# A graph layer's edge stage on blocks of 128 nodes instead of 64, one block per turn

## The chip, the core and the metric

The kernel runs on one core of a Trainium2 chip. A core has five engines that run side by side, each with its own queue of instructions: TensorE (PE, matmuls; PEld is its weight load), VectorE (DVE), ScalarE (ACT), GpSimd (POOL) and SyncE (SP), which here only issues DMAs. They wait for each other on semaphores. SBUF is the memory that the engines work from, PSUM holds what TensorE makes, HBM is the large memory outside. The metric is the device time of the whole program in microseconds (us).

## What is computed

A graph has 6250 nodes of 256 values, and 206250 edges sorted by their target `dst`. The layer is, cut to what matters here:

```python
h = (xn @ W.T).reshape(n, 8, 32)                       # xn: layernorm of x
alpha = sum(h[src] * a_src) + sum(h[dst] * a_dst)      # per edge and head
enc = relu(edge_attr @ edge_W.T + edge_b)
alpha = leaky(alpha + sum(enc * h[dst]))
ex = exp(alpha - segment_max(alpha, dst)[dst])
gnn = segment_sum(h[src] * ex / segment_sum(ex, dst)[dst], dst) + bias
x = x + gnn + mix(xn)                                  # mix: a linear attention over all nodes
out = x + experts(layernorm(x))                        # 8 experts of three layers, a softmax gate
```

## The kernel before

The program is unrolled and runs in stages, with all engines meeting between them.

**start** (`stage_start`): layernorm, h, and the plan of the edges. Per tile of 128 nodes SyncE stores the rows of h with their source scores to HBM (`src_rows`, L351) and two halves of `parts` (`dst_parts`, L358), in which h is split into three bf16 parts, so that bf16 matmuls give it back exactly. The plan cuts the sorted edges into groups of 256 (GE) and the nodes into blocks; a step is one group against one block, and where a group runs over a block's end the step is repeated for the next block.

**kv and mix**: the linear attention. In between GpSimd gathers some of the edges' rows ahead of time.

**edges** (`stage_edges`): 452 turns (D) of 512 edges. A turn d belongs to window d // 8. In turn tau the engines do, each in the order written here:

- TensorE: `spread_out(tau)`, h[dst] for 512 edges into `ps_d`, from the block's `table` and the one-hot matrix `hot` (L1652: the third bf16 part, 64 rows; L1656: the first two parts, 128 rows); `encode(tau+1)`, the edge features (L1641); `aggregate(tau-12)`; `reduce(tau)`, the sum over a head's 32 values (L1669).
- VectorE: `multiply(tau)` (L1837, two halves), the next `hot` (L1826), `weigh(tau-11)` (L1920, the rows by their exponentials), and `add(tau-12)` (L1913, into `sums`). In the first four turns of a window also the softmax work of the window before: scores, two scans, the chain of running maxima, the shift, the rescaling.
- ScalarE: `rectify(tau+1)` (L1734), `put_back(tau-12)` (L1787), the source scores (L1745), the exponentials into the rows (L1771), and the one-hot matrices `hot_e` of 128 edges by 64 nodes for the aggregation (L1779, L1781).
- GpSimd gathers the rows of the sources (L1629), SyncE loads tables, relative indices and features.

A block has 64 nodes (WN), so `sums` has 98 blocks, and each is two partial sums, one on the lower 64 partitions and one on the upper. A turn may meet two blocks, one for each of its two steps (`sub`). So a turn loads two tables, and its aggregation is in two parts. For step 0, unless the turn opens a window, TensorE first copies the block's sums into PSUM with an identity matmul (L1688), accumulates on them, and ScalarE copies the result back (L1787). For step 1 VectorE adds (L1913). The matmuls of a step write partitions 0 to 63 and 64 to 127 (L1692). The order is kept by one counter, `added`: the aggregation of a turn waits for both sums of the turn before, and the add of step 1 for the copy back of step 0.

**combine** (`stage_combine`, the head of the last part): per tile TensorE adds the partial sums (`band_sum`, L2223) of two blocks into one tile of 128 nodes. VectorE divides by the denominators (L2063, L2068, L2073), adds the rest (L2082) and takes the statistics (L2086); ScalarE normalises; TensorE turns the tile (L2207) and makes the router's logits (L2213), 21 tiles later. The experts' weights are loaded into the place of `sums` once it is read.

**experts** (`stage_experts`): dense matmuls.

## Time and profile before

| | us |
|---|---|
| median of 3 runs | 4003.45 (4001.85 to 4003.85) |
| the profiled execution, first to last instruction | 4846.5 |
| of it: start (0 to 190) | 190 |
| kv and mix (190 to 1038) | 848 |
| edges (1038 to 3704) | 2666 |
| combine (3704 to 3827) | 123 |
| experts (3827 to 4847) | 1020 |

### The profile page before, as it was taken

The numbers are of one execution on the slowest core, as the hardware profiler recorded it, in microseconds if no ns is written. First come the engines' busy times: TensorE is split into PE (matmuls) and PEld (weight loads), VectorE is DVE, ScalarE is ACT, GpSimd is POOL, SyncE is SP. The second block draws the span as 40 slices with busy tenths as digits, with TensorE's granted clock in tenths as the row PEclk, the third lists the DMA queues.
The fourth block names the chain that finished last, engine by engine and source line by source line (L and its number), as shares of the span: only waits on it lengthen the run. The fifth ranks groups of instructions, "written<-read, shape, count | busy, mean of one in ns | idle before, by whom it ended". The sixth has DMA issues, their size and how long they took to land. (4 is left out here: it accounts for less than half of the span.)

```text
span 4846.5 us, 80424 instructions
## 1 busy us (share of the span) xinstructions
PE 4087.7 (84%) x22764; PEld 1897.1 (39%) x22765; DVE 2700.2 (56%) x5470; ACT 2291.3 (47%) x6074; POOL 1780.1 (37%) x1859
## 2 busy tenths in 40 slices
PE   5699988957888887788887878878887999999999
PEld 3333322312333333333333333333333666666666
DVE  7566723336666666676666666667666333333333
ACT  4444445524555555555555555555554433333332
POOL 3255555644454445444444444445440000000000
PEclk8799989976888888888888887888887799999999
DMA  7555556655555555555555555555552100000000
GB/s 216 160 165 162 164 177 201 210 156 154 161 168 165 158 165 164 162 168 168 159 162 152 163 157 161 162 159 168 164 162 67 61 8 1 8 8 8 8 8 8
DMA packets 378173, 629.74 MB, mean 130 GB/s; under 512 B 83912, under 2 KB 245063, under 8 KB 377536
## 3 DMA queue, kind: packets, MB, share of 16 engines
q1 hardware_dynamic: 277266, 356.80, 23.4%
q0 software_dynamic: 93408, 257.23, 19.5%
q10 hardware_dynamic: 7104, 11.01, 0.7%
q8 instruction: 179, 2.93, 0.2%
q14 instruction: 216, 1.77, 0.1%
HBM read 520.59 MB, written 104.12 MB: 129 GB/s over the span
## 5 line engine op out<-in xcount | busy, mean ns | idle before, releaser
L1629 POOL DMA_INDIRECT s_rows<-scratch_src_rows,s_idx_w x1312 | 1257.6, 959 | 1367.6 <-PE s_ps_a L1692 563.3
L1837 DVE SCALAR_TENSOR_TENSOR s_enc<-s_enc,s_a_dst,s_ps_d 128x512 f32<-128x512 f32 x904 | 634.9, 741 | 313.3 <-DMA p_feats<-in_edge_f,p_tcol_i 160.8
L1734 ACT ACTIVATE s_enc<-s_ps_f 128x1024 f32<-128x1024 f32 x452 | 459.5, 1017 | 516.6 <-remote 265.5
L1692 PE MATMUL s_ps_a<-s_rows,s_hot_e 128*64 128x264 f32 x3616 | 647.1, 490 | 44.9 <-DVE s_rows L1920 32.4
L2285 DVE SCALAR_TENSOR_TENSOR kx_y_all<-e_ps_o,kx_gate,kx_y_all 128x256 f32 (+1 forms) x392 | 173.5, 480 | 684.2 <-PE e_ps_o L2340 684.2
L1920 DVE TENSOR_TENSOR s_rows<-s_rows,s_ps_x 128x1024 f32<-128x1024 f32 x452 | 545.7, 1207 | 13.6 <-ACT s_a_w L1765 8.7
L1688 PE MATMUL s_ps_a<-ke_sums,k_ident 128*128 x790 | 341.0, 520 | 217.1 <-DVE ke_sums L1913 123.6
L1913 DVE TENSOR_TENSOR ke_sums<-s_ps_a,ke_sums 128x264 f32 x509 | 218.3, 429 | 505.3 <-remote 263.9
L1669 PE MATMUL s_ps_s<-s_enc,s_head_sum 128*32 128x256 f32 x3616 | 353.7, 469 | 152.9 <-DVE s_enc L1837 121.2
L1779 ACT ACTIVATE s_hot_e<-k_iota_row,s_rel_w 128x64 f32<-128x64 f32 x1808 | 480.5, 339 | 0.0
L1787 ACT COPY ke_sums<-s_ps_a 128x264 f32 x395 | 148.6, 376 | 552.5 <-remote 337.8
L2299 ACT ACTIVATE ke_sums<-e_ps,kx_b,kx_g 128x448 f32<-128x448 f32 x224 | 162.1, 724 | 512.9 <-PE e_ps L2319 512.9
L1692 PEld LDWEIGHTS s_ps_a<-s_rows,s_hot_e 128*64 128x64 f32 x3616 | 263.0, 163 | 360.2 <-issue 264.5
L2319 PE MATMUL e_ps<-kx_xT,ke_sums 128*128 (+1 forms) x896 | 347.9, 542 | 6.2 <-PEq L180 6.2
L2340 PE MATMUL e_ps_o<-ke_sums 128*128 128x256 f32 x1568 | 347.6, 379 | 0.0
L2329 PE MATMUL e_ps<-ke_sums 128*128 128x448 f32 x896 | 345.9, 539 | 0.0
L1641 PE MATMUL s_ps_f<-s_feat,k_w_rows 30*128 30x512 bf16 x904 | 304.0, 419 | 27.7 <-DMA s_feat<-scratch_step_parts 14.6
L1656 PE MATMUL s_ps_d<-s_hot,s_table 128*128 128x256 bf16 x1808 | 321.7, 308 | 0.0
L2340 PEld LDWEIGHTS e_ps_o<-ke_sums 128*128 128x128 f32 x1568 | 297.7, 190 | 58.6 <-issue 20.9
L1091 POOL DMA_INDIRECT n_rows<-scratch_src_rows,n_idx x248 | 235.0, 947 | 207.0 <-PE n_ps_g L948 107.5
L1195 POOL DMA_INDIRECT m_rows<-scratch_src_rows,m_idx x248 | 235.7, 951 | 174.7 <-issue 64.6
L1688 PEld LDWEIGHTS s_ps_a<-ke_sums,k_ident 128*128 128x128 f32 x790 | 139.0, 220 | 373.5 <-issue 370.6
(280 smaller groups left out, 5259.0 us busy)
## 6 DMA issues: line engine op xcount, KB each, us to landing
s_table<-scratch_dst_parts SPq DMA_DIRECT2D x904, 96.0 KB
s_rows<-scratch_pre_rows SPq DMA_DIRECT2D x124, 528.0 KB
s_relb<-scratch_rel_rows SPq DMA_DIRECT2D x226, 256.0 KB
scratch_pre_rows<-n_rows SPq DMA_DIRECT2D x62, 528.0 KB
scratch_pre_rows<-m_rows SPq DMA_DIRECT2D x62, 528.0 KB
s_rows<-scratch_src_rows,s_idx_w POOLq DMA_INDIRECT x1312
s_feat<-scratch_step_parts SPq DMA_DIRECT2D x226, 54.0 KB
s_pen_w<-scratch_pen_rows SPq DMA_DIRECT2D x228, 48.1 KB
```

The source lines that it names most:

```text
L1629: pool.indirect_dma_start(out=rows[:, d % R, m, :], out_offset=None, in_=scr["src_table"], in_offset=bass.IndirectOffsetOnAxis(ap=idx_w[:, ...
L1656: last = PE.matmul(ps_d[:, c, sub * GE:(sub + 1) * GE], table[:, u, sub, c * P:(c + 1) * P], hot[:, v, sub * GE:(sub + 1) * GE], start=Fal ...
L1669: last = PE.matmul(ps_s[32 * b:32 * (b + 1), :], head_sum[:, 28 - 4 * k:60 - 4 * k], enc[:, d % 2, c, sub * GE:(sub + 1) * GE], start=(k = ...
L1688: PE.matmul(ps_a[:, 0, 0:SRC_W], keep["ident"][:], sums[:, bass.ds(j, 1), :].rearrange("p o w -> p (o w)"), start=True, stop=False, skip_g ...
L1692: last = PE.matmul(ps_a[t * WN:(t + 1) * WN, sub, 0:SRC_W], hot_e[:, d % 3, 2 * sub + t, :], rows[:, d % R, 2 * sub + t, :], start=(sub == ...
L1734: A.activation(enc[:, d % 2], ps_f[:], ACT.Relu).then_inc(enc_made, 1)
L1779: A.activation(hot_e[:, d % 3, m, :], keep["iota_row"][:, 0:WN], ACT.Abs, bias=rel_w[:, w % 3, k * TD + m:k * TD + m + 1]).then_inc(dist_m ...
L1837: V.scalar_tensor_tensor(out=enc[:, d % 2, c, :], in0=enc[:, d % 2, c, :], scalar=a_dst[:, c:c + 1], in1=ps_d[:, c, :], op0=ALU.add, op1=A ...
L1920: V.tensor_tensor(v, v, by.unsqueeze(3).to_broadcast([P, TD, H, HD]), ALU.mult).then_inc(weighed, 1)
L2319: last = nc.tensor.matmul(ps[q][:, 0:W], w["W1"][:, e, c, m * P:(m + 1) * P], keep["xT"][:, c, bass.ds(i * 2 * W + hf * W, W)], start=(c = ...
L2329: last = nc.tensor.matmul(ps[q][:, 0:W], w["W2"][:, e, c, m * P:(m + 1) * P], h1[:, c, hf * W:(hf + 1) * W], start=(c == 0), stop=(c == 1))
L2340: last = nc.tensor.matmul(ps_o[q][:, r, :], h2[:, c, b * P:(b + 1) * P], w["Wo"][:, e, c, :], start=(c == 0), stop=(c == 1))
```

## The change

WN becomes 128. A block is then a tile of 128 nodes; there are 49 of them. The plan takes pairs of groups, 512 edges, against one block, so both steps of a turn have the same block. A turn then does the following.

- It loads one table of 128 x 768 bf16 values, which start stores with one DMA per tile.
- `spread_out` is six matmuls of 128 rows over 512 columns, three parts for each half of the 256 values.
- The aggregation is four matmuls onto all 128 partitions, into one of two PSUM banks in turn, with no identity matmul and no copy back, and one add by VectorE. It waits for the sum of the turn but one before.
- `hot_e` is 128 edges by 128 nodes.
- `reduce` of a turn comes one turn later, behind the next `spread_out`.

In combine the `band_sum` matmuls go, the division reads `sums` in place with the denominators inverted for seven tiles at once, the logits follow without the lag, and the weights have their own place in SBUF. In start the plan has half as many entries to make. The output's computation is the same.

```diff
-WN = P // 2
+WN = P
...
-                        for b in range(2):
-                            sp.dma_start(scr["dst_parts"][2 * d + b].rearrange("c n w -> n c w"), parts[b * WN:(b + 1) * WN, d % RP]).then_inc(d_stored[d % RP], 16)
+                        sp.dma_start(scr["dst_parts"][d], parts[:, d % RP].rearrange("p c w -> p (c w)")).then_inc(d_stored[d % RP], 16)
...
-    NJ = 2 * NT
-    T = -(-E // GE)
-    D = -(-(T + NJ - 1) // 4) * 2
+    NJ = NT
+    T = 2 * -(-E // (2 * GE))
+    D = -(-(T // 2 + NJ - 1) // 2) * 2
...
                     for c in range(2):
                         wait(pe, prod_made[c], d)
-                    for sub in range(2):
-                        for c in range(2):
-                            PE.matmul(ps_d[:, c, sub * GE:(sub + 1) * GE], table[c * 64:(c + 1) * 64, u, sub, C:HALF],
-                                      hot[c * 64:(c + 1) * 64, v, sub * GE:(sub + 1) * GE], start=(sub == 0), stop=False, skip_group_check=True)
-                    for c in range(2):
-                        for sub in range(2):
-                            last = PE.matmul(ps_d[:, c, sub * GE:(sub + 1) * GE], table[:, u, sub, c * P:(c + 1) * P],
-                                             hot[:, v, sub * GE:(sub + 1) * GE], start=False, stop=True, skip_group_check=True)
-                        last.then_inc(spread[c], 1)
+                        PE.matmul(ps_d[:, c, :], table[:, u, c, C:HALF], hot[:, v, :], start=True, stop=False)
+                        PE.matmul(ps_d[:, c, :], table[:, u, 1, c * P:(c + 1) * P], hot[:, v, :], start=False, stop=False)
+                        PE.matmul(ps_d[:, c, :], table[:, u, 0, c * P:(c + 1) * P], hot[:, v, :], start=False, stop=True).then_inc(spread[c], 1)
...
-                    wait(pe, added, 2 * d)
-                    if k > 0:
-                        PE.matmul(ps_a[:, 0, 0:SRC_W], keep["ident"][:], sums[:, bass.ds(j, 1), :].rearrange("p o w -> p (o w)"),
-                                  start=True, stop=False, skip_group_check=True)
-                    for sub in range(2):
-                        for t in range(TG):
-                            last = PE.matmul(ps_a[t * WN:(t + 1) * WN, sub, 0:SRC_W], hot_e[:, d % 3, 2 * sub + t, :], rows[:, d % R, 2 * sub + t, :],
-                                             start=(sub == 1 or k == 0), stop=True, skip_group_check=True)
-                        last.then_inc(summed[sub], 1)
+                    wait(pe, added, d - 1)
+                    for m in range(TD):
+                        last = PE.matmul(ps_a[:, d % 2, 0:SRC_W], hot_e[:, d % 3, m, :], rows[:, d % R, m, :], start=(m == 0), stop=(m == TD - 1))
+                    last.then_inc(summed, 1)
...
                     if tau < D:
                         spread_out(tau)
+                    if 0 < tau <= D:
+                        reduce(tau - 1)
...
-                    if tau < D:
-                        reduce(tau)
...
-                def put_back(d):
-                    w, k = win(d)
-                    j = act.value_load(turns_w[0:1, w % 4, KS + 2 * k:KS + 2 * k + 1], min_val=0, max_val=NJ - 1)
-                    act.wait_ge(summed[0], d + 1)
-                    A.copy(sums[:, bass.ds(j, 1), :].rearrange("p o w -> p (o w)"), ps_a[:, 0, 0:SRC_W]).then_inc(added, 1)
...
-                    V.tensor_tensor(y, ps_a[:, sub, 0:SRC_W], y, ALU.add).then_inc(added, 1)
+                    V.tensor_tensor(y, ps_a[:, d % 2, 0:SRC_W], y, ALU.add).then_inc(added, 1)
...
-                        for b in range(2):
-                            last = PE.matmul(ps_n[u][b * WN:(b + 1) * WN, 0:SRC_W], band_sum[:], sums[:, 2 * i + b, :], start=True, stop=True)
-                        last.then_inc(banded[u], 1)
-                    if 0 <= i - LATE < NT:
-                        turn(i - LATE)
-                    if 0 <= i - LATE - 1 < NT:
-                        logits(i - LATE - 1)
+                        turn(i)
+                    if i > 0:
+                        logits(i - 1)
...
-                        weights=flat[:, 0:NE].rearrange("p (m e c n) -> p m e c n", m=3, e=EXPERTS, c=2),
+                        weights=kit.sb("weights", [P, 3, EXPERTS, 2, C]),
```

TensorE in an ordinary turn of the edge stage, from encode on: before (`s_ps_f` edge features, `s_ps_a` the aggregation, `s_ps_s` the reduced scores, `s_ps_d` the spread h[dst]).

```order
L1641 MATMUL s_ps_f<-s_feat,k_w_rows 128x512 x2
L1682 TENSOR_LOAD s_turns_w
L1682 ISA x2
L1688 ISA
L1688 MATMUL s_ps_a<-ke_sums,k_ident 128x264
L1692 MATMUL s_ps_a<-s_rows,s_hot_e 64x264 x4
L1669 MATMUL s_ps_s<-s_enc,s_head_sum 32x256 x4
L1652 MATMUL s_ps_d<-s_hot,s_table 128x256 x4
L1656 MATMUL s_ps_d<-s_hot,s_table 128x256 x4
```

The same engine and place after the change.

```order
L1636 MATMUL s_ps_d<-s_hot,s_table 128x512
L1637 MATMUL s_ps_d<-s_hot,s_table 128x512
L1638 MATMUL s_ps_d<-s_hot,s_table 128x512
...
L1649 MATMUL s_ps_s<-s_enc,s_head_sum 32x256 x4
L1627 MATMUL s_ps_f<-s_feat,k_w_rows 128x512 x2
L1665 MATMUL s_ps_a<-s_rows,s_hot_e 128x264 x4
```

The identity matmul and its register load are gone, the four matmuls of the aggregation are 128 wide, the reduction stands behind the spread of the next turn, and the spread is twice three matmuls of 512 columns (the second three left out).

ScalarE in an ordinary turn, before.

```order
L1734 ACTIVATE s_enc<-s_ps_f 128x1024
L1785 TENSOR_LOAD s_turns_w
L1785 ISA x2
L1787 ISA
L1787 COPY ke_sums<-s_ps_a 128x264
L1745 COPY s_a_win<-s_rows 128x2x4x4
L1771 COPY s_rows<-s_a_w 128x32
L1779 ACTIVATE s_hot_e<-k_iota_row,s_rel_w 128x64 x4
L1781 ACTIVATE s_hot_e<-s_hot_e,s_one 128x256
```

And after.

```order
L1706 ACTIVATE s_enc<-s_ps_f 128x1024
L1717 COPY s_a_win<-s_rows 128x2x4x4
L1743 COPY s_rows<-s_a_w 128x32
L1751 ACTIVATE s_hot_e<-k_iota_row,s_rel_w 128x128 x4
L1753 ACTIVATE s_hot_e<-s_hot_e,s_one 128x512
```

The copy back and its register load are gone; the one-hot rows are twice as wide.

## Rows read from the trace of the kernel before

**Rows 1.** the head of the page: the profiled span.

```profile
span 4846.5 us, 80424 instructions
```

**Rows 2.** stages by stretch: us, busy by engine (instructions), clock, DMA share, GB/s.

```profile
0.00:190.00 190.00, 96.67 (x372) 70.53 (x372) 119.11 (x334) 85.68 (x230) 51.84 (x51) 0.80 0.69 195
...
1038.00:3704.00 2666.00, 2137.97 (x13340) 860.27 (x13340) 1761.08 (x3352) 1449.86 (x4297) 1256.76 (x1312) 0.81 0.55 158
3704.00:3827.00 123.00, 94.18 (x491) 64.40 (x492) 68.29 (x313) 45.46 (x110) 0.00 (x0) 0.65 0.34 114
3827.00:4847.00 1020.00, 1013.75 (x3360) 638.56 (x3359) 328.79 (x784) 324.11 (x448) 0.00 (x0) 1.00 0.02 6
```

**Rows 3.** timeline of TensorE, two turns: start, duration, engine, line, operation, count [idle].

```profile
1964.06 0.39 PE L1652 MATMUL s_ps_d<-s_hot,s_table 64*128 64x256 bf16 x4
1964.38 0.61 PE L1656 MATMUL s_ps_d<-s_hot,s_table 128*128 128x256 bf16 x4
1964.92 0.60 PE L1641 MATMUL s_ps_f<-s_feat,k_w_rows 30*128 30x512 bf16 x2
1965.46 0.71 PE L1688 MATMUL s_ps_a<-ke_sums,k_ident 128*128 x2
1966.10 1.11 PE L1692 MATMUL s_ps_a<-s_rows,s_hot_e 128*64 128x264 f32 x8
1967.14 0.64 PE L1669 MATMUL s_ps_s<-s_enc,s_head_sum 128*32 128x256 f32 x8
1967.71 0.39 PE L1652 MATMUL s_ps_d<-s_hot,s_table 64*128 64x256 bf16 x4
...
1971.36 0.28 PE L1652 MATMUL s_ps_d<-s_hot,s_table 64*128 64x256 bf16 x2
```

**Rows 4.** the same stretch as Rows 2, for those two turns.

```profile
1964.00:1971.00 7.00, 7.00 (x56) 2.94 (x56) 5.68 (x12) 5.08 (x13) 2.43 (x3) 1.00 0.53 161
```

**Rows 5.** timeline of VectorE, a window's first turn and the next one's begin.

```profile
2993.11 1.40 DVE L1837 SCALAR_TENSOR_TENSOR s_enc<-s_enc,s_a_dst,s_ps_d 128x512 f32<-128x512 f32 x2
...
2997.93 1.40 DVE L1837 SCALAR_TENSOR_TENSOR s_enc<-s_enc,s_a_dst,s_ps_d 128x512 f32<-128x512 f32 x2
```

**Rows 6.** the groups of instructions: busy us, mean ns | idle before, releaser.

```profile
L1779 ACT ACTIVATE s_hot_e<-k_iota_row,s_rel_w 128x64 f32<-128x64 f32 x1808 | 480.5, 339 | 0.0
...
L1688 PE MATMUL s_ps_a<-ke_sums,k_ident 128*128 x790 | 341.0, 520 | 217.1 <-DVE ke_sums L1913 123.6 <-issue 66.2 <-ACT s_hot_e L1781 11.3
...
L1781 ACT ACTIVATE s_hot_e<-s_hot_e,s_one 128x256 f32<-128x256 f32 x452 | 229.5, 508 | 14.7
L1913 DVE TENSOR_TENSOR ke_sums<-s_ps_a,ke_sums 128x264 f32 x509 | 218.3, 429 | 505.3 <-remote 263.9 <-ACT ke_sums L1787 137.1 <-PE s_ps_a L1692 94.8
...
L1787 ACT COPY ke_sums<-s_ps_a 128x264 f32 x395 | 148.6, 376 | 552.5 <-remote 337.8 <-PE s_ps_a L1692 166.5 <-issue 47.5
...
L1722 PE MATMUL s_ps_x<-s_perm,s_prob 128*128 128x128 f32 x228 | 47.7, 340 | 1.0 <-ACT s_prob L1758 1.0
L1676 PE MATMUL s_ps_s<-k_ident,s_a_win 128*128 128x128 f32 x228 | 44.2, 325 | 36.6 <-issue 35.2 <-ACT s_a_win L1745 1.4
```

**Rows 7.** timeline of TensorE in combine: a tile, two late ones, the experts' first.

```profile
3749.85 0.67 PE L2223 MATMUL b_ps_n<-ke_sums,b_band_sum 128*64 128x264 f32 x4
...
3751.16 0.67 PE L2223 MATMUL b_ps_n<-ke_sums,b_band_sum 128*64 128x264 f32 x4
...
3796.22 0.67 PE L2207 MATMUL b_ps_t<-k_ident,kx_xT 128*128 128x128 f32 x2
...
3797.40 0.67 PE L2207 MATMUL b_ps_t<-k_ident,kx_xT 128*128 128x128 f32 x2
...
3826.62 4.07 PE L2319 MATMUL e_ps<-kx_xT,ke_sums 128*128 128x448 f32 x5 [6.16 <-PEq L180]
```

**Rows 8.** timeline of SyncE in start: one tile.

```profile
158.24 0.59 SPq L351 DMA_DIRECT2D scratch_src_rows<-p_hs  x1
158.87 1.25 SPq L358 DMA_DIRECT2D scratch_dst_parts<-p_parts  x2
```

230 lines of the change are left out of this document (96 added, 134 removed).

## The prediction

> **What bounds the kernel now.** I read the profile in this order: the table of stages, then inside the long stage the order of TensorE's instructions with their starts, then the groups of instructions, then the waits. The stages first [rows 2]: of the 4846.5 us of the profiled span [rows 1], the edge stage takes 2666 us, the head of the last part (combine) 123 us, the experts 1020 us, and everything ahead of the edges 1038 us. The edge stage is 452 turns long, with 12 more turns in which only the last sums are made. Per turn TensorE is busy 2137.97/452 = 4.73 us, VectorE 3.90, ScalarE 3.21 and GpSimd 2.78, at a mean granted clock of 0.81. So TensorE is the fullest engine, VectorE next, and neither is full by this view.
>
> The second view says why. Where nothing disturbs the stage, two ordinary turns stand back to back with TensorE's group starts at 1964.06, 1967.71 and 1971.36 us: 3.65 us each, the engine busy without a gap, at granted clock 1.00 [rows 3, 4]. So an ordinary turn is bound by TensorE. A turn in which a window of eight turns hands over its softmax work is different: in the one from 2993.11 to 2997.93 VectorE works without a gap for 4.82 us (the two products, the scores, the two scans, the weights, the add, the ends) [rows 5]. Four turns of a window carry such work, four do not. The undisturbed edge stage is then about (4 x 4.8 + 4 x 3.65)/8 = 4.23 us per turn.
>
> **The profiled execution and the runs.** The runs' median is 4003.45 us, 843 us below the span of the profiled execution; no other time of that execution is given. The experts' 1020 us are TensorE busy 99% at clock 1.00, so they can't shrink. If all 843 us are lost in the edge stage, the runs' edge stage is 2666 - 843 = 1823 us, or, less some 30 us for its last 12 turns (an estimate), 3.97 us per turn. If every stage but the experts shrinks alike, by (4003 - 1020)/(4846 - 1020) = 0.78, it is 2079 us, 4.53 per turn. The rows' own 4.23 lies between and gives 1912 us. I take that as the base and keep 3.97 and 4.53 as its bounds. The sum below is made in undisturbed microseconds and set on the median; made on the profiled span it would add the same microseconds there, blurred by whatever that execution lost.
>
> **The change, part by part.** The number of turns stays 452: before, (806 + 97)/4 rounded up, times 2; after, (403 + 48)/2 rounded up, times 2. What changes is what a turn does.
>
> 1. The spread matmuls (L1652, L1656). Now four of 64 rows and four of 128 rows, each over 256 columns, which take 1964.06 to 1964.92 = 0.86 us [rows 3]. The first four run in pairs: four in 0.32 us against 0.54 for the four of full height. After the change each block has 128 nodes, so six full-height matmuls over 512 columns. One of the latter has to cost twice a 256-column one: 0.54/4 x 2 = 0.27 at most; the two 512-column matmuls of L1641 take 0.54 with what follows, 0.27 each. Without the gap at a group's end it is 512/2.4 = 0.213. So 6 x 0.213 = 1.28 and one such gap of 0.12: 1.40 us (bounds 1.28 and 1.62). Added: 0.54 us.
>
> 2. The aggregation (L1688, L1692). Now the identity matmul that brings the sums back into PSUM, 0.64 us (1965.46 to 1966.10), and four matmuls of 64 columns of output that run in pairs, 1.04 us to 1967.14 [rows 3]. After: four matmuls over all 128 outputs, each the width of the identity one. Two of today's in a pair share the time of one, so the streaming doubles: each pass over 264 columns is 0.22 us, two passes each, 8 x 0.22 = 1.76, and the 0.16 to 0.20 us by which both groups of today exceed their streaming: 1.96 (bounds 1.76 and 2.56, four times the identity's 0.64). Against 1.68: added 0.28 us; in the one turn of eight without an identity matmul 0.92.
>
> 3. encode and reduce cost what they do, 0.54 and 0.57 us [rows 3]. reduce moves behind the next spread, so it no longer waits for VectorE's products; queued behind it stand encode, the aggregation and the rest of TensorE's turn.
>
> TensorE's ordinary turn becomes 1.40 + 0.57 + 0.54 + 1.96 = 4.47 us. To it comes the window's own work: L1676 and L1722 are (44.2 + 47.7)/57 = 1.6 us per window [rows 6], the three small ones 0.4 by estimate, so 0.25 per turn. Together 4.72, say 4.7 us per turn, 2124 us.
>
> 4. VectorE: one add of 0.43 us goes where a window begins (57 of 509 [rows 6]), 0.05 per turn; 3.85 stay. It has 0.85 us of air per turn, 6.8 per window, against the 4 x (4.8 - 3.65) = 4.6 that the window's work adds. In the first window turn it runs over, but the products of the next turn are due only at the spread after that, and the sums' add only after the aggregation. So that work, which bounds half of today's turns, hides behind TensorE. Were half of it not hidden, 0.3 us per turn, 130 us, would be added.
>
> 5. ScalarE: the copy back, 0.376 us x 395 [rows 6], goes. The four one-hot rows of 64 become 128 wide (L1779, 480.5 us in all, 1.06 per turn), and the rectifier of them 512. Between nothing and twice: at most 1.06 + 0.51 [rows 6] more, 3.21 - 0.33 + 1.57 = 4.45 us per turn, still under 4.7. Nothing on the path.
>
> 6. The chain that goes: add, identity matmul, copy, add. It cost TensorE 123.6 us waiting for the add, and VectorE 137.1 us waiting for the copy [rows 6]. Both lie in turns that wait anyway for VectorE's window work or in stalled ones; in the ordinary turns of rows 3 they are nil. The gain is contained in the base of 4.23, which the new TensorE turn replaces as a whole. Late next is TensorE itself.
>
> 7. SyncE loses one register load and one table load per turn; the bytes per turn (2 x 96 KB, now 1 x 192 KB) stay. The gather (GpSimd, 2.78 us busy) keeps its distance. Nothing.
>
> Edge stage: 2124 - 1912 = +212 us.
>
> 8. The head (combine). The band-sum matmuls and the two small VectorE steps per tile go; the router's transposes no longer lag 21 tiles; the experts' weights have a place of their own and load at once. Before, a tile took 3751.16 - 3749.85 = 1.31 us, and the last 20 tiles ran behind at 3797.40 - 3796.22 = 1.18 us each, at half clock, before the first expert matmul at 3826.62 [rows 7]. After: some 10 us until the first group of seven is normalised, 49 x 1.18 = 58 us at worst, a tail of 7.5 us: 76 to 83 of today's 123 us. Take -40 (bounds -30 and -55).
>
> 9. The start. Its queue on SyncE issues without a pause, a tile taking 0.6 us for the rows of h and 1.25 us for two stores of parts [rows 8]. One store instead of two saves up to 0.62 x 49 = 30 us, and the rows written are twice as long; VectorE is busy 119 of 190 us there [rows 2], so some of it stays. Take -25 (bounds 0 and -45).
>
> Sum: 212 - 40 - 25 = +147, that is **4150 us**, 3.7% slower. With the base at 3.97 the edge term is +330 and the time 4268; at 4.53 it is +77 and 4015.
>
> **Rivals.** (a) *The gaps between groups shrink.* Today's turn has 0.8 us more than its streaming: the turn streams 0.64 + 0.43 + 0.44 + 0.88 + 0.43 = 2.8 us (columns over 2.4 GHz, concurrent ones counted once) and takes 3.65. If that belongs to the changes between matmuls of 64 rows, 128 rows, 64 and 32 columns, two of which go, the new turn comes near its own streaming, 3.95 + 0.1, with the window's 0.25 about 4.3: +30 us, with the head and start 3968 us, faster. Against it: the encode group and the identity matmul, of full width, show gaps as large (0.11 and 0.20). The Trainium skill, TensorEngine Tiling (Array Packing), Key Properties, says that switching the tiling mode drains TensorE; by that rule this rival holds. The rows don't separate a drain from an unhidden weight load, so it gets 0.08.
>
> (b) *The chain is the bound.* If the stage hangs on the sums' way through PSUM and ScalarE rather than on TensorE, the change takes off the 123.6 + 137.1 us of both waits and the time is 4003 - 261 - 65 = 3677 at best; TensorE's streaming of 4.2 us per turn stops it at about 1912 - 1898 = 14 below, 3924. It decides only if TensorE's new turn is under 4.2. Against it are rows 3. Chance 0.06.
>
> (c) *Even.* Base at its upper bound, 4.53, and TensorE's turn at 4.65: +54 - 65, 3992 to 4010. Chance 0.05.
>
> (d) *The clock falls.* The profile has TensorE at 0.81 in this stage and at 1.00 in the experts, where it never idles [rows 2]. After the change it should idle less. If VectorE's window work still stops it long enough to fall to 1.2 GHz once per window for some 7 us, 3.5 us are lost per window, 0.43 per turn: +195, 4345 us. Chance 0.09.
>
> **How the numbers follow.** The forecast, TensorE-bound at 4.55 to 4.85 us per turn, has 0.72 and spans 4050 to 4290. Range: 3960 to 4290 takes in (a) and (c) and leaves out (b), (d) and a little of the forecast's own tails, under 0.2 together. A measurement of this kernel can tell about 0.2% (8 us) from no change. Faster (a, b) 0.14; same 0.05; slower 0.81.
>
> **What would show it.** In the profile after: the six 512-column matmuls from first start to the next group 1.3 to 1.5 us and the aggregation 1.8 to 2.1 at clock 1.00; the mean clock of the stage above 0.90; TensorE's busy share above 90%, with VectorE's waits for PSUM grown; combine at 75 to 90 us, the start at 145 to 190. The prediction is wrong if the ordinary turn at full clock is under 4.2 us (a), if TensorE waits for VectorE in every window (d), or if the window turns of before cost more in the runs than 4.8 us, which lifts the base.

## The result and the profile after

The changed kernel takes **4091.75 us** (median of 4 runs, 4090.84 to 4093.77) against 4002.65 for the kernel before (4 runs, 3986.76 to 4003.85): a ratio of 1.0239, 95% interval 1.0217 to 1.0261. It is slower, by 89 us where 147 were forecast. Its profiled execution took 4091.89 us with a span of 4090.1, so this profile is one of the timed runs.

The first view is the page of the changed kernel: its span and the engines' busy time (us, share of the span, instructions).

```profile
span 4090.1 us, 69358 instructions
...
PE 3903.1 (95%) x20859; PEld 2146.1 (52%) x20859; DVE 2669.1 (65%) x5320; ACT 2364.7 (58%) x5679; POOL 1790.6 (44%) x1858
```

The stages by stretch, with the columns of [rows 2]: start, the two stages between, edges, combine, experts.

```profile
0.00:164.00 164.00, 87.36 (x356) 63.02 (x356) 114.84 (x328) 86.28 (x230) 50.64 (x50) 0.85 0.73 226
164.00:489.00 325.00, 304.65 (x2998) 129.48 (x2998) 285.09 (x409) 179.66 (x738) 235.47 (x248) 0.96 0.70 212
489.00:861.00 372.00, 344.92 (x2207) 117.90 (x2207) 133.59 (x280) 205.99 (x252) 238.24 (x252) 0.97 0.69 220
861.00:2968.00 2107.00, 2091.15 (x11644) 1139.06 (x11644) 1744.01 (x3291) 1523.08 (x3902) 1266.21 (x1309) 0.99 0.69 199
2968.00:3070.00 102.00, 61.33 (x294) 57.75 (x294) 62.49 (x228) 45.16 (x110) 0.00 (x0) 0.52 0.41 137
3070.00:4090.00 1020.00, 1013.73 (x3360) 638.84 (x3360) 329.10 (x784) 324.58 (x448) 0.00 (x0) 1.00 0.02 6
```

In the edge stage TensorE is busy 2091 of 2107 us at a granted clock of 0.99. It is the bound of the stage, with nothing left over. An ordinary turn on TensorE and the next one's begin, the answer to [rows 3]:

```profile
1982.32 0.38 PE L1636 MATMUL s_ps_d<-s_hot,s_table 128*128 128x512 bf16 x1
...
1983.71 0.64 PE L1649 MATMUL s_ps_s<-s_enc,s_head_sum 128*32 128x256 f32 x8
1984.28 0.60 PE L1627 MATMUL s_ps_f<-s_feat,k_w_rows 30*128 30x512 bf16 x2
1984.81 2.05 PE L1665 MATMUL s_ps_a<-s_rows,s_hot_e 128*128 128x264 f32 x8
1986.69 0.38 PE L1636 MATMUL s_ps_d<-s_hot,s_table 128*128 128x512 bf16 x1
```

By the starts: spread 1.39 us (1982.32 to 1983.71), reduce 0.57, encode 0.53, aggregation 1.88; the turn takes 1986.69 - 1982.32 = 4.37 us. At least 96% of the turns at each place of a window repeat their time within 0.01 us. The four turns of a window that carry window work add only their own matmuls: by their places in the window the turns take 5.02, 4.53, 4.52, 5.23 and four times 4.37 us, 4.60 on average, 0.22 of it the window's work.

Who waits for whom: groups of the changed page (busy us, mean ns | idle before, releaser), and the largest waits of all engines between 950 and 2900 us (us, times, longest), behind GpSimd's own 453.3 us of "issue":

```profile
L1665 PE MATMUL s_ps_a<-s_rows,s_hot_e 128*128 128x264 f32 x3616 | 925.6, 399 | 2.9 <-DVE s_rows L1879 2.9
...
L1872 DVE TENSOR_TENSOR ke_sums<-s_ps_a,ke_sums 128x264 f32 x452 | 193.3, 428 | 218.2 <-PE s_ps_a L1665 212.9
```

```profile
ACT s_enc L1706 <- PE s_ps_f L1627: 332.3, 314, 1.3
POOL s_rows L1615 <- PE s_ps_a L1665: 306.1, 120, 4.3
DVE ke_sums L1872 <- PE s_ps_a L1665: 198.0, 243, 1.5
```

ScalarE, GpSimd and VectorE wait for TensorE; before its 3616 aggregation matmuls TensorE stood idle 2.9 us in all. In [rows 6] TensorE waited 123.6 us for VectorE's add, and VectorE 137.1 us for the copy back.

**Two levels of time.** One fact is needed for all that follows. All the runs below are from three other chips (numbered 3, 5 and 6), and there the kernel before takes about 4780 us (medians 4783.88 of 19 runs, 4778.94 of 12 and 4779.6 of 7, every run between 4761 and 4820) and the changed kernel 4554. The profile of before in [rows 1] (span 4846.5 us) looks like those and not like the 4003 us of its runs. I call the two levels two kinds of chip. That it is the chip is an inference: the record doesn't number the chip of the result, and something that went with the time of the runs is not excluded. No trace of the kernel before at its 4003 us exists. What differs is told under the experiments.

### The profile page after: what moved, and what is told of

Its sections match the earlier page's. It is cut to its first block and busy times, and to the rows that moved or that the text cites. A ratio compares the mean times of both kernels' runs of the same rounds, so it can differ in the third digit from the quotient of the medians.

```text
span 4090.1 us, 69358 instructions
## 1 busy us (share of the span) xinstructions
PE 3903.1 (95%) x20859; PEld 2146.1 (52%) x20859; DVE 2669.1 (65%) x5320; ACT 2364.7 (58%) x5679; POOL 1790.6 (44%) x1858
## 5 line engine op out<-in xcount | busy, mean ns | idle before, releaser
L1665 PE MATMUL s_ps_a<-s_rows,s_hot_e 128*128 128x264 f32 x3616 | 925.6, 399 | 2.9 <-DVE s_rows L1879 2.9
L1665 PEld LDWEIGHTS s_ps_a<-s_rows,s_hot_e 128*128 128x128 f32 x3616 | 650.9, 190 | 239.4 <-issue 140.3
L1751 ACT ACTIVATE s_hot_e<-k_iota_row,s_rel_w 128x128 f32<-128x128 f32 x1808 | 577.2, 392 | 2.3 <-PE s_ps_a L1665 2.3
L2261 PE MATMUL e_ps<-kx_xT,kx_weights 128*128 (+1 forms) x896 | 347.5, 541 | 6.1 <-PEq L180 6.1
L1636 PE MATMUL s_ps_d<-s_hot,s_table 128*128 128x512 bf16 x904 | 345.2, 382 | 5.7 <-DVE s_hot L1786 3.1
L2282 PE MATMUL e_ps_o<-kx_weights,ke_sums 128*128 128x256 f32 x1568 | 347.6, 379 | 0.0
L2271 PE MATMUL e_ps<-ke_sums,kx_weights 128*128 128x448 f32 x896 | 345.9, 539 | 0.0
L1638 PE MATMUL s_ps_d<-s_hot,s_table 128*128 128x512 bf16 x904 | 345.1, 382 | 0.0
L1637 PE MATMUL s_ps_d<-s_hot,s_table 128*128 128x512 bf16 x904 | 344.8, 381 | 0.0
L1753 ACT ACTIVATE s_hot_e<-s_hot_e,s_one 128x512 f32<-128x512 f32 x452 | 326.3, 722 | 14.7
L2282 PEld LDWEIGHTS e_ps_o<-kx_weights,ke_sums 128*128 128x128 f32 x1568 | 297.8, 190 | 58.6 <-issue 21.0
L1649 PE MATMUL s_ps_s<-s_enc,s_head_sum 128*32 128x256 f32 x3616 | 290.6, 393 | 0.0
```

Source lines behind the costliest of these rows:

```text
L1636: PE.matmul(ps_d[:, c, :], table[:, u, c, C:HALF], hot[:, v, :], start=True, stop=False)
L1637: PE.matmul(ps_d[:, c, :], table[:, u, 1, c * P:(c + 1) * P], hot[:, v, :], start=False, stop=False)
L1638: PE.matmul(ps_d[:, c, :], table[:, u, 0, c * P:(c + 1) * P], hot[:, v, :], start=False, stop=True).then_inc(spread[c], 1)
L1665: last = PE.matmul(ps_a[:, d % 2, 0:SRC_W], hot_e[:, d % 3, m, :], rows[:, d % R, m, :], start=(m == 0), stop=(m == TD - 1))
L1751: A.activation(hot_e[:, d % 3, m, :], keep["iota_row"][:], ACT.Abs, bias=rel_w[:, w % 3, k * TD + m:k * TD + m + 1]).then_inc(dist_made, 1)
L2261: last = nc.tensor.matmul(ps[q][:, 0:W], w["W1"][:, e, c, m * P:(m + 1) * P], keep["xT"][:, c, bass.ds(i * 2 * W + hf * W, W)], start=(c = ...
```

## The experiments

Turns are measured as the distance between the starts of two spread groups on TensorE. "Undisturbed" is the 10th percentile of it at each of the eight places in a window, averaged over the places; "lost" is the sum by which the stage's 451 distances exceed it. Where stops are frequent this length is a low estimate: for the changed kernel the eight places add up to 36.8 us and the best whole window of after_again takes 37.4, but for the kernel before they add up to 32.8 to 33.4 us in three traces, and no whole window takes less than 39.9.

### The kernel before, looked at again

> The kernel before, unchanged, for a profile that can be set beside the one after. The one after has a span of 4090 us for a time of 4092, so the 843 us by which the profile of before exceeded its runs belonged to that one execution. Theory 1 (the base was too low): the stages ahead of the edges take about 885 us (the 860 of after and 25 for the second store), combine 123 to 145, experts 1020, and the edge stage what is left, 1960 to 1990 us, 4.30 to 4.37 per turn, not the 4.23 of the prediction. Theory 2 (the base of 4.23 stands): edges 1912 us and the stages ahead of them 950.

4784.92 us, so it can't decide between the two theories on the base. Its stages, the columns of [rows 2] (the edge stage is cut here at the first `band_sum` matmul; the last sum of the edges ended at 3634.1):

```profile
0.00:190.00 190.00, 96.60 (x372) 72.72 (x372) 118.96 (x337) 85.91 (x230) 51.95 (x51) 0.79 0.68 195
190.00:601.00 411.00, 346.67 (x3002) 139.51 (x3002) 286.57 (x408) 175.42 (x738) 236.22 (x248) 0.95 0.54 168
601.00:1036.00 435.00, 369.01 (x2211) 125.40 (x2211) 133.52 (x282) 206.82 (x252) 240.20 (x252) 0.91 0.59 189
1036.00:3644.00 2608.00, 2100.49 (x13338) 848.42 (x13334) 1760.73 (x3349) 1452.49 (x4297) 1259.67 (x1308) 0.82 0.58 162
3644.00:3763.00 119.00, 102.50 (x491) 69.42 (x491) 67.77 (x313) 44.31 (x109) 0.00 (x0) 0.60 0.30 101
```

The engines' own work is as large as in [rows 2] (VectorE 1760.73 against 1761.08 us); what varies is idle time. One such hole, the timelines of three engines and of SyncE's issues:

```profile
1131.89 1.11 PE L1692 MATMUL s_ps_a<-s_rows,s_hot_e 128*64 128x264 f32 x8
1140.04 1.08 PE L1669 MATMUL s_ps_s<-s_enc,s_head_sum 128*32 128x256 f32 x8 [7.04 <-DVE s_enc L1837]
...
1138.49 1.41 DVE L1837 SCALAR_TENSOR_TENSOR s_enc<-s_enc,s_a_dst,s_ps_d 128x512 f32<-128x512 f32 x2 [8.09 <-DMA p_feats<-in_edge_f,p_tcol_i]
...
1138.50 1.02 ACT L1734 ACTIVATE s_enc<-s_ps_f 128x1024 f32<-128x1024 f32 x1 [7.08 <-remote]
...
1138.62 1.47 SPq L1600 DMA_DIRECT2D s_table<-scratch_dst_parts  x2
```

and the engines' busy time in it:

```profile
1132.99:1138.45 5.46, 0.01 (x2) 0.00 (x0) 0.00 (x0) 0.00 (x0) 2.85 (x3) 0.76 0.71 174
```

TensorE, VectorE and ScalarE stand, SyncE's DMA issues pause from 1135.7 to 1138.6, GpSimd gathers on until 1136.7, and then VectorE and ScalarE start within 0.01 us of each other. I call this a joint stop. By the program VectorE waits here for the spread, ScalarE for the encoding, and SyncE's next table load for the second half of the spread, so all three wait for TensorE. By the records of the matmuls these were done by about 1131.3. But the trace has the updates of their semaphores at 1138.40 and 1138.44 (spread) and 1138.48 (encoding), 7 us later, and the three engines go on at once then. ("DMA p_feats" in VectorE's line is the view's guess; in this stage that semaphore is the spread's.)

The other traces say the same. From the start of the last encoding matmul to the update of its semaphore it is 0.39 us in the profile of the result (448 updates recorded in the stage, none over 0.64 us). In after_again 76 of 384 come more than 2 us after it, in before_again 102 of 371, the latest 21 and 17 us. VectorE's and ScalarE's own updates (products, encoding rectified) come 0.01 us after their instruction in all of these traces. So the stops sit between TensorE's matmuls, as recorded, and their semaphores. Whether the matmuls themselves ran late (their ends are modelled) or only their updates is not shown.

### The same once more, on another chip

> The kernel before once more, for a profile without the joint stops that its first two show (all engines but GpSimd stand still for some microseconds at a time, and a span of 4784 to 4847 us). If it comes out near 4003 us: theory 1, start and linear attention 885 us, edges 1960 to 1990 us (4.30 to 4.37 per turn); theory 2, edges 1912 us. If it is near 4780 again, the stops belong to the chip and not to the execution.

4789.94 us, the edge stage 2633.8 against 2608.5 us (both up to the first `band_sum` matmul). The joint stops are no accident of one chip or one run. Without the stage's first turns the excess of each turn over its undisturbed length correlates between the three traces of before with 0.47 to 0.54: to a good part the same turns are hit. The start takes 190.8 us (190.1 before), and from the last sum of the edges to the experts it is 134.7 us (128.8 in before_again, 122.8 in the trace of [rows 2]).

### reduce behind the next spread, alone

```diff
                     if tau < D:
                         spread_out(tau)
+                    if 0 < tau <= D:
+                        reduce(tau - 1)
...
-                    if tau < D:
-                        reduce(tau)
```

> Of the change only its order: in the kernel before, the reduction of a turn stands behind the next turn's spread, and the one-hot matrix ahead of the scores. Theory 1: an ordinary turn is TensorE's own work, 3.65 us, and stays; the window's turns are VectorE's, and stay; within 0.5% of before. Rival: TensorE's wait for the products is what stretches the window's turns beyond 4.8 us; then up to 0.2 us per turn, 90 us, 2.2% faster.

4776.2 us, ratio 0.998 (0.995 to 1.001): no difference that can be measured, as theory 1 had it. The edit has a second part, not shown above: VectorE's one-hot matrix goes ahead of the scores, as in the changed kernel. Together they do nothing for the kernel before.

### No copy back, alone

The identity matmul (L1688) and the copy (L1787) go; VectorE adds both halves' sums from PSUM, two adds a turn on blocks of 64.

```diff
-                    if k > 0:
-                        PE.matmul(ps_a[:, 0, 0:SRC_W], keep["ident"][:], sums[:, bass.ds(j, 1), :].rearrange("p o w -> p (o w)"),
-                                  start=True, stop=False, skip_group_check=True)
...
-                    d = tau - LAG - 1
-                    if 0 <= d and win(d)[1] > 0:
-                        put_back(d)
...
                     if tau >= LAG + 1:
+                        add(tau - LAG - 1, 0)
                         add(tau - LAG - 1, 1)
```

> Of the change only the chain: in the kernel before, both steps' sums are added by VectorE, so the identity matmul (0.64 us of TensorE in seven turns of eight) and ScalarE's copy back go, and VectorE makes 395 adds more of 0.43 us. Theory 1 (TensorE bounds the four ordinary turns, VectorE the four window turns): ordinary turns fall from 3.65 to VectorE's 3.5, window turns grow by 0.43; +0.14 us per turn, 60 us, 1 to 2% slower. Rival b of the prediction (the chain add, identity matmul, copy, add is the bound): 100 us or more faster.

4739.27 us, ratio 0.9901 (0.9864 to 0.9938).

> The kernel before with both steps' sums added by VectorE, no identity matmul, no copy back, again. Beside joint stops it was 0.990 of before. Theory 1 (ordinary turns bound by TensorE, window turns by VectorE): on undisturbed turns 3.5 instead of 3.65 and 5.2 instead of 4.8 us, 1 to 2% slower. Rival: the chain add, identity matmul, copy, add costs more than TensorE's 0.64 us; then 1% or more faster here too.

4735.44 us, 0.9913 (0.9888 to 0.9937), on the other chip. So the part is worth 1%, some 43 us, where theory 1 expected 1 to 2% slower both times and the rivals 100 us or 1% and more. Its edge stage:

```profile
1022.00:3587.00 2565.00, 1949.33 (x12550) 768.95 (x12552) 1914.99 (x3744) 1320.91 (x3902) 1261.73 (x1308) 0.76 0.58 165
```

Against before_third_look, on the same chip, TensorE loses 164 us of busy time (2112.87 there) and VectorE gains 154 (1760.85). The medians differ by 43 us. The rival that the chain of add, identity matmul, copy and add was the bound priced it at both waits of [rows 6], 261 us, or at 100 and more in the text on record; it did not come. The test is not a clean one, since what the chain gives back stands beside 154 us of new work for VectorE.

### The changed kernel with reduce at the turn's end

```diff
-                    if 0 < tau <= D:
-                        reduce(tau - 1)
...
+                    if tau < D:
+                        reduce(tau)
```

> The changed kernel with the reduction back at the end of its own turn. Theory 1: TensorE is now busy throughout, VectorE's products of a turn are made long before its end; within 0.5% of the changed kernel in ordinary turns, and in window turns TensorE waits for products again: up to 1% slower than the changed kernel (ratio to before 1.024 to 1.035). Rival: the later reduction is what keeps TensorE full; then 3% or more slower than the changed kernel.

4858.85 us, ratio to before 1.0142 (1.007 to 1.0214), below what theory 1 had.

> The changed kernel with the reduction at the end of its own turn, again. Beside joint stops it was 1.014 of before. If TensorE is full in the changed kernel, the ratio to before is 1.024 to 1.035 on undisturbed turns; if the later reduction is what keeps it full, 1.05 or more.

4874.47 us, 1.0186 (1.0145 to 1.0228), again below both numbers on record. Where no stop falls, its ordinary turn is this:

```profile
1701.93 0.39 PE L1636 MATMUL s_ps_d<-s_hot,s_table 128*128 128x512 bf16 x1
...
1703.33 0.60 PE L1627 MATMUL s_ps_f<-s_feat,k_w_rows 30*128 30x512 bf16 x2
1703.86 2.05 PE L1665 MATMUL s_ps_a<-s_rows,s_hot_e 128*128 128x264 f32 x8
1705.84 0.64 PE L1649 MATMUL s_ps_s<-s_enc,s_head_sum 128*32 128x256 f32 x8
1706.41 0.39 PE L1636 MATMUL s_ps_d<-s_hot,s_table 128*128 128x512 bf16 x1
```

4.48 us against 4.37. The groups are the same; from the aggregation's start to the next group's it is 1.98 us where reduce follows and 1.88 where the spread does. Averaged over the places of a window the undisturbed turn is 4.67 against 4.60: the order of reduce is worth 0.07 us a turn, 32 us of the stage. In the ordinary turn the whole difference, 0.10 us, stands behind the aggregation.

### The changed kernel itself, beside the kernel before

> The changed kernel once more, beside the kernel before on the chip of this call. If the chip is one on which before takes about 4780 us and its engines stop jointly now and then: after_reduce_at_end took 1.014 and 1.019 of before there, and after_no_third_part 0.963. Theory 1 (TensorE bounds the new turn; the stops cost both kernels alike, some 780 us): 4003.45 -> 4091.75 is +89 us, so 4780 + 89 = 4869, ratio 1.018, edge stage about 2770 us, and moving reduce back to the turn's end costs nothing (after_reduce_at_end equal to it within 0.3%). Rival (the order of reduce matters in the new kernel): after_again is 0.5 to 1% faster than after_reduce_at_end, 4825 to 4850. Theory 2 (stops are gaps between a turn's engines and the new kernel is less exposed to them): under 4780, ratio below 1.00. If this chip has no stops: 4092 and 1.022.

4553.6 us against 4779.6: ratio **0.9507** (0.9469 to 0.9545). On these chips the sign is the other one. Its stages:

```profile
0.00:163.00 163.00, 91.80 (x356) 66.08 (x356) 115.02 (x330) 86.55 (x230) 50.62 (x50) 0.82 0.73 228
163.00:581.00 418.00, 360.75 (x3002) 143.35 (x3002) 286.79 (x408) 177.45 (x738) 236.18 (x248) 0.93 0.53 165
581.00:1007.00 426.00, 357.35 (x2207) 121.63 (x2207) 134.09 (x280) 206.80 (x252) 239.59 (x252) 0.94 0.60 192
1007.00:3452.00 2445.00, 2199.86 (x11644) 1173.20 (x11644) 1727.61 (x3291) 1507.54 (x3902) 1264.80 (x1309) 0.95 0.59 172
3452.00:3554.00 102.00, 61.33 (x294) 57.75 (x294) 62.50 (x228) 45.16 (x110) 0.00 (x0) 0.52 0.40 137
```

Start and combine are what they were on the first chip, within 2 us, and the experts take 1019.9 us. Its undisturbed turn is 4.60 us here as well, place by place to 0.01. What is added is lost time: 93 + 54 us in the two stages between, 338 in the edge stage. Theory 1 of the text on record falls: the stops do not cost both kernels alike. The number of theory 2 holds, a ratio below 1.00, but the runs below speak against its mechanism. The rival on the order of reduce expected 0.5 to 1% (4825 to 4850 us), and the gap to the version with reduce at the turn's end is some 310 us, over 6%. Those two ran on different chips, so they are compared over the kernel before, which takes the same within 0.1% on all three. Only 32 us of the gap are in the turns: that version loses 608 and 630 us in the edge stage to stops, this one 328.

### The changed kernel without a third of the spread

Two of the six spread matmuls are left out, so the attention logits lack a part.

```diff
-                        PE.matmul(ps_d[:, c, :], table[:, u, c, C:HALF], hot[:, v, :], start=True, stop=False)
-                        PE.matmul(ps_d[:, c, :], table[:, u, 1, c * P:(c + 1) * P], hot[:, v, :], start=False, stop=False)
+                        PE.matmul(ps_d[:, c, :], table[:, u, 1, c * P:(c + 1) * P], hot[:, v, :], start=True, stop=False)
```

> The changed kernel without the third bf16 part of h[dst] (it leaves out two of the six spread matmuls of a turn; its results are less exact). If TensorE bounds every turn of the changed kernel, each matmul of 512 columns costs its 0.22 us: 452 x 0.43 = 195 us less, 3900 us where the changed kernel takes 4092 (0.974 of before). If VectorE is close behind (3.87 us busy per turn, window turns above), a part only: 100 to 150 us less. If something else bounds: nothing.

4602.96 us, ratio to before 0.9629 (0.9564 to 0.9695). The ordinary undisturbed turn is 3.94 us instead of 4.37 and the mean over the window 4.17 instead of 4.60: two matmuls of 0.216 us each, the turn shrinks by just what TensorE sheds. The stage does not: 2459.5 us against after_again's 2445.2, with 534 us lost instead of 328. So none of the 195 us expected is seen in the program's time; against the kernel before it does worse than the changed kernel, 0.9629 to 0.9507.

### The changed kernel with the aggregation in pairs

```diff
-                        last = PE.matmul(ps_a[:, d % 2, 0:SRC_W], hot_e[:, d % 3, m, :], rows[:, d % R, m, :], start=(m == 0), stop=(m == TD - 1))
+                        last = PE.matmul(ps_a[(m % 2) * 64:(m % 2 + 1) * 64, d % 2, 0:SRC_W], hot_e[:, d % 3, m, 0:64], rows[:, d % R, m, :],
+                                         start=(m < 2), stop=(m >= 2), skip_group_check=True)
```

> The changed kernel with the aggregation of a turn brought back to matmuls of 64 columns of output that run in pairs, as before the change: only the first 64 of the block's 128 nodes are summed, so part of the computation is left out (the other nodes' sums). The aggregation group, 1.884 us with the change, should take about 1.0 us (the two pairs of before took 1.04). Theory (TensorE bounds every turn): 0.85 us less on 452 turns, minus what the window turns don't give: between 300 and 385 us less than after_again, about the sum of both terms' price. after_no_third_part, 0.5 us less on TensorE per turn, gained about 260 us in 452 turns (0.57 a turn). Rival (below 3.9 us of TensorE per turn VectorE at 3.86 takes over): the gain stops at (4.60 - 3.95) x 452 = 290 us or less, and VectorE is above 90% busy in the edge stage.

4470.12 us against 4553.6 of the changed kernel on the same chip, 84 us less where 300 to 385 were expected. From one turn of it and the next one's spread:

```profile
1996.23 0.60 PE L1627 MATMUL s_ps_f<-s_feat,k_w_rows 30*128 30x512 bf16 x2
1996.76 1.11 PE L1665 MATMUL s_ps_a<-s_rows,s_hot_e 128*64 128x264 f32 x8
1997.80 0.39 PE L1636 MATMUL s_ps_d<-s_hot,s_table 128*128 128x512 bf16 x1
...
2001.34 0.39 PE L1636 MATMUL s_ps_d<-s_hot,s_table 128*128 128x512 bf16 x1
```

The aggregation takes 1.04 us instead of 1.88, as in [rows 3], and the ordinary turn 3.54 instead of 4.37. So the wider aggregation costs 0.84 us of an ordinary turn. Averaged over the window it is less, 3.91 against 4.60, since the second turn of a window doesn't shrink at all (4.67 against 4.53; TensorE waits there for VectorE's ends of the segments); 0.69 us over 451 turns would be 310 us. The time fell by only 84 us, with 552 us lost instead of 328. The rival with VectorE as the bound is not settled by this: VectorE is busy 1728 of 2357 us, 73% and not above 90%, but that is 3.82 us a turn, nearly the whole of the 3.91, and the best whole window of the trace takes 35.5 us, 4.44 a turn, with VectorE busy 85% of it.

### One store per tile, in the kernel before

```diff
-                        for b in range(2):
-                            sp.dma_start(scr["dst_parts"][2 * d + b].rearrange("c n w -> n c w"), parts[b * WN:(b + 1) * WN, d % RP]).then_inc(d_stored[d % RP], 16)
+                        sp.dma_start(scr["dst_parts"][2 * d:2 * d + 2].rearrange("b n c w -> (b n) (c w)"), parts[:, d % RP].rearrange("p c w -> p (c w)")).then_inc(d_stored[d % RP], 16)
...
-                        sp.dma_start(table[:, u, sub, :], row(scr["dst_parts"], j).rearrange("o c n w -> (o c n) w")).then_inc(table_in[u], 16)
+                        sp.dma_start(table[:, u, sub, :], row(scr["dst_parts"], j).rearrange("o n c w -> (o c) n w")).then_inc(table_in[u], 16)
```

> The kernel before with one change of the new one alone: the two blocks of a node tile lie as rows (node, 2, 192) in memory, so that SyncE issues one store per tile where it issued two; the table loads of the edge stage read the same bytes in another order (runs of 768 bytes in place of 384). Theory (SyncE's issuing bounds the start, as priced in term 9): start 190.5 -> 163 to 166 us, total -25 us, ratio 0.994 to 0.995; edge stage unchanged within 0.5%. Rival (the 26 us came from the wider blocks, the tile's own work or the shorter setup): start stays at 188 to 191, ratio 1.000. A second rival: the loads of a block in runs twice as long speed the edge stage too: ratio below 0.99.

5283.56 us, ratio **1.105** (1.1008 to 1.1091). The start went from 190.1 to 168.5 us, nearly the 163 to 166 expected. The edge stage, expected unchanged, lost 530 us:

```profile
1004.00:4142.00 3138.00, 2371.65 (x13338) 927.09 (x13334) 1781.19 (x3349) 1471.60 (x4297) 1246.72 (x1304) 0.74 0.45 135
```

The loads read the same bytes in the same number of packets, 128 of 768 bytes each (384 values of 2 bytes; the text on record has 384 and 768 bytes for the rows, half of what they are). But the rows of a load no longer lie end to end; each is now 1536 bytes from the next, and the load is written in another form, in the trace's record a destination of [1,128] elements of 768 bytes where it was [128,1]. Between 1400 and 2800 us the trace shows what that does. A packet takes as long as before (36 ns median). In before_again 6.2 table packets are under way at a time on average, 22 at most, and a load's 128 packets are through in 0.67 us. In before_one_store it is 1.9, 4 at most, and 2.8 us a load; table packets are under way in 1037 of the 1400 us, against 438. SyncE's instructions fill 85% of the time, against 59%; a table load is issued in 0.62 us (median) where it took 0.34, the load of `rel` in 2.28 where it took 0.43, although that one was not touched. Here it is in SyncE's timeline, before_one_store:

```profile
2000.69 5.67 SPq L1599 DMA_DIRECT2D s_table<-scratch_dst_parts  x3
2006.41 2.67 SPq L1585 DMA_DIRECT2D s_relb<-scratch_rel_rows  x1
2009.13 0.76 SPq L1587 DMA_DIRECT2D s_feat<-scratch_step_parts  x1
```

So each load runs with few packets at a time and takes four times as long, the queue that issues the loads is held up, and the turns follow. In the edge stage the load is the only edit, so it is the cause. Two things changed with it: the distance of the rows, and the form, whose source is now 2 x 64 rows where it was 128. The packets go by twos, which fits the form; no run takes the two apart.

> The kernel before with two parts of the change that don't widen a block: the sums of both halves are added from PSUM by VectorE, with no copy back by ScalarE and no identity matmul (0.991 of before by itself in two runs), and one store of the parts per tile (expected 0.994 to 0.995). If the two are independent: 0.985 to 0.986, 4780 -> 4710, the start at 163 to 166 us; and this would be the fastest kernel of the study with nothing left out. If the VectorE-bound edge stage takes back what the store gives: 0.990.

5282.06 us, 1.1052 (1.1007 to 1.1097): the same as with the store alone, where 4710 were expected. With the table loads as the bound, the 43 us of the missing copy back are worth nothing. Of the kernels with the whole computation the changed one is the fastest on the three chips; on the first only it and the kernel before were run.

## Why the prediction was right, and where its terms were off

The forecast was 4150 us and slower; it came out as 4092 and slower, inside the range. TensorE bounds the new turn, the window's work hides behind it, ScalarE and GpSimd stay off the path. That is what the profile after shows, and the two kernels that take matmuls out of the turn support it: each shortened the ordinary undisturbed turn by the time of the matmuls (0.43 and 0.84 us). The program's time on those chips did not follow, since more was lost to stops.

**Part 1, the spread:** 1.39 us measured, 1.40 predicted. **Part 3:** 0.57 and 0.53, as predicted.

**Part 2, the aggregation:** 1.88 us, 1.96 predicted. Mis-sized: I gave the one group of four the excess of both of today's groups. A group has one gap, 1.884 - 1.76 = 0.12 us. The 0.08 us too much are most of the 0.10 us by which the ordinary turn (4.37 against 4.47) was too long.

**The window's own matmuls:** 0.22 us a turn, 0.25 predicted. With the rounding from 4.72 to 4.7 the turn came to 4.7 where 4.60 was measured: 45 us of the stage.

**Part 4, VectorE:** right. From 1961.8 to 1975.6 us it works off the scores, scans and products of one window almost without a gap, and TensorE's turns stay what they are.

**Part 6, the chain:** right that its waits are no gain to be added. before_no_copy_back took it away, with 154 us more for VectorE, and got 43 us, not 261.

**Part 7, SyncE:** "nothing" was right for this change: in the profile after 6.6 table packets are under way at a time, and a load's 128 packets are through in 1.3 us. before_one_store shows that it isn't nothing by nature: the table loads alone can become the bound.

**Part 8, combine:** mis-sized. Predicted -40 (bounds -30 and -55) and 76 to 83 us after. From the last sum of the edges to the experts' first matmul, the stretch that the prediction's 123 us are, the three traces of before have 122.8, 128.8 and 134.7 us and the two of after 102.8 and 103.1, so -20 to -32 (before only on the other chips). The step that was off is "some 10 us until the first group of seven is normalised". From the first instruction of the head it is 21, from the last sum 22:

```profile
2969.08 0.21 DVE L2010 TENSOR_SCALAR b_inv<-ke_sums 128x56 f32<-128x56 f32 x1 [1.31 <-PEq L180]
...
2974.29 0.42 DVE L2027 TENSOR_TENSOR kx_y_all<-ke_sums,kx_y_all 128x256 f32<-128x256 f32 x1 [3.67 <-DMA kx_y_all<-scratch_x_mix]
...
2989.92 1.09 PE L2156 MATMUL b_ps_t<-k_ident,kx_xT 128*128 128x128 f32 x4 [22.74 <-ACT kx_xT L2125]
...
3061.13 0.67 PE L2156 MATMUL b_ps_t<-k_ident,kx_xT 128*128 128x128 f32 x2
...
3062.30 0.67 PE L2156 MATMUL b_ps_t<-k_ident,kx_xT 128*128 128x128 f32 x2
...
3070.59 1.08 PE L2261 MATMUL e_ps<-kx_xT,kx_weights 128*128 128x448 f32 x1 [6.11 <-PEq L180]
```

VectorE waits 3.67 us for the residual's load and needs some 1.1 us for each tile. The seven are done at about 2982, but their statistics then go step by step between the tiles of the next group until 2989.1, another 6 us and more; TensorE begins at 2989.92. From there on it is mostly 1.17 us a tile at half clock, as predicted from [rows 7].

**Part 9, the start:** 164.6 us against the 190.1 to 191.0 of the traces of before, -26; predicted -25. SyncE issues one store a tile:

```profile
130.16 0.32 SPq L350 DMA_DIRECT2D scratch_src_rows<-p_hs  x1
130.52 0.47 SPq L356 DMA_DIRECT2D scratch_dst_parts<-p_parts  x1
132.19 0.32 SPq L350 DMA_DIRECT2D scratch_src_rows<-p_hs  x1
```

The pauses between the tiles say that it no longer issues without a stop, as it did in [rows 8]. before_one_store found 21.6 us of the 26 with the store alone.

**The base** has only a residual. The stages between take 844 us in after_again and 820 to 851 in the three traces of before, no clear difference, so I take their 697 us of the first chip for both; no run shows that for the kernel before. Then its edge stage is 4002.65 - 1.8 (around the span) - 190.5 - 697 - 129 - 1020 = 1964 us, and 1964 - 35 for the last sums is 1929, 4.27 us a turn, where I had 4.23. The edge term was about +142 us instead of +212: some 50 of the difference are the new turn, the rest the base or what else hides in the residual. The terms -26, -26 and +142 make +90; that they meet the measured 89 is no proof, since the base was worked out from it. The start came out as priced. That the forecast came within 58 us is in part luck: by this account the edge term was 70 us too high and the head's 14 too low, and the two partly cancel. The low side of the turns of before can be seen: the 10th percentiles at the eight places in before_again are 4.78, 4.59, 3.80, 4.61, 3.89, 4.45, 3.65 and 3.65 (mean 4.18; 4.10 and 4.14 in the other two traces). So not four and four turns but three near 4.7, two at 3.65, and three between or mixed; the count of four and four from [rows 3] and [rows 5] was too simple, though its mean came near.

**The rivals.** (a), the gaps shrink, had a turn near 4.05 without the window's work; 4.37 was measured. The gaps after the change are 0.09 after the spread (0.309 for its last matmul against 0.216), 0.14 after reduce, 0.10 after encode and 0.12 after the aggregation. They stayed.

The Trainium skill, TensorEngine Tiling (Array Packing), Key Properties, has a change of the tiling mode drain TensorE. The trace does not show it as a price of its own: from the spread to reduce, into matmuls of 32 columns, costs 0.309 us, and from the spread to encode, 128 columns as before, 0.311. Only behind the aggregation is there a difference, 0.22 into reduce against 0.12 into the spread. 

(b) decided only if TensorE's new turn were under 4.2 us; it is 4.60. (d) did not come: the clock is 0.99 in the stage. On the other chips it is lower, 0.95 with the change and 0.82 before, where TensorE also stands idle for 245 and some 500 us of the stage.

**What the prediction did not see.** It read the 843 us between the span and the runs as losses that any execution of the kernel before might have, and set the sum on the median. That was the right choice for the result's chip. But the losses are not spread alike over kernels, and by more than the change is worth: by the measure above 1.5 to 1.6 us a turn in before (658 and 724 us in before_again and before_third_look), 0.7 in the changed kernel, 1.3 to 1.4 in the changed kernel with reduce in another place. So the forecast holds for the chip of the result; on the other three the sign is wrong, and the prediction has no term for it.

## What to carry to other kernels

Where an engine is to become the bound, count its turn from the starts of its groups, give every group one gap of 0.1 us, and add the matmuls of the rarer work; that was right to 3% here. A latency at the head of a stage (first load, first group, first statistics) wants its own count from rows, not a round figure. Before the shape of a DMA is changed, count how many of its packets run at a time in the trace. Before a difference of some per cent is explained by the edit, look at whether undisturbed turns of both kernels differ by as much: here a moved reduce changed the mean turn by 0.07 us, 32 us in all, and the program by some 310.

## What the runs showed that I had not expected

The joint stops. On three chips TensorE, VectorE and ScalarE stand together, SyncE soon too, and go on together, and single turns lose up to 18 us; on the chip of the result the changed kernel has none (4 turns in the trace are more than 0.3 us too long, against 164 in after_again). In the stop shown above, what ends it is the update of semaphores of TensorE's matmuls, microseconds after their records. Of the some 110 idle times over 3 us that VectorE and ScalarE have in the edge stage of after_again, about 90 end with such a semaphore; the largest group by far is ScalarE's for the encoding, 63 times and 364 us in all. Start, combine and experts of the changed kernel are the same on both, 163 to 165, 103 and 1020 us.

Two traces of one kernel have their stops to a good part in the same turns (correlation of the excess per turn, without the stage's first turns: about 0.64 for the kernel with reduce at the end, 0.5 without copy back and for before). Between kernels it is less: 0.44 for the changed kernel and the one with the aggregation in pairs, 0.27 without a third of the spread, 0.02 and 0.00 for the one with reduce at the end. So the places go with the program as it is laid out. The amount does not follow TensorE's work: 328 us lost in the edge stage with all of it, 534 with two matmuls fewer a turn, 552 with the aggregation halved.

The median time of a DMA packet on either queue is the same on both kinds of chip (65 and 164 ns in the changed kernel). The turns of after_again in which a packet of instructions is fetched are 0.8 to 1.0 us too long on average, all turns 0.7; in before_again it is 1.8 against 1.5. A longer turn is also likelier to hold such a packet, so this shows no cause. One more thing goes with the stops: the traces of the three chips lack many semaphore updates (384 recorded for 451 encodings in after_again, 448 in the profile of the result). All these runs have a recorded span, so whether the recording has a part in the stops can't be said. The cause stays open.

The second surprise is that another form of a load, with the same bytes and the same number of loads and packets, made a kernel 10% slower: rows of 768 bytes, 1536 bytes apart instead of end to end, went two at a time instead of six.
